# The second score matmul on 128 rows, with projections two pairs of heads ahead

## The reference

```
mod = (silu(c) @ wmod)                          # six vectors per batch
h = layernorm(x) * (1 + ca) + sa
q, k, v = h @ qkv_w.T                           # 16 heads of 64
scores = q k^T / 8 + bias[head, q, k]           # T5 buckets of the distance
x = x + ga * (softmax(scores) v) @ o_w.T
h = layernorm(x) * (1 + cb) + sb
x = x + gb * (routed experts(h) + shared expert(h))   # 160 experts, top 8 by sigmoid
```

## Time and profile before

| | |
|---|---|
| runs (median, range) | 1110.45 us (1110.03 to 1115.24) |
| profiled execution, first to last instruction | 1108.8 us |
| busy: PE, PEld, DVE, ACT | 1067.8, 695.6, 774.9, 729.6 us |
| mean granted TensorE clock | 0.981 |
| attention | about 26 to 615 us |
| experts | about 653 us to the end |

### The profile page before, as it was taken

How to read it: one execution, slowest core, us unless ns; L and a number is a source line. 1 busy time by engine, 2 the same in 40 slices (tenths; PEclk the granted TensorE clock), 3 DMA queues, 4 the chain that set the end, 5 groups by cost and what they waited for, 6 DMA issues and landing times.

```text
span 1108.8 us, 16554 instructions
## 1 busy us (share of the span) xinstructions
PE 1067.8 (96%) x4720; PEld 695.6 (63%) x4720; DVE 774.9 (70%) x1356; ACT 729.6 (66%) x1216; POOL 0.2 (0%) x4
## 2 busy tenths in 40 slices
PE   5999999999999999999999779999999999999998
PEld 2555555555555555555555347788888888888886
DVE  5655555655555555555554558899999999999997
ACT  3566666566665666666665456777777778777775
POOL 0000000000000000000000000000000000000000
PEclk8699999999999999999999899999999999999999
DMA  7651323132231313231321039999999999999993
GB/s 220 193 148 39 77 59 75 44 71 58 75 76 38 76 38 76 57 76 39 76 56 41 1 108 218 218 220 218 218 220 219 218 217 221 218 218 218 221 218 85
DMA packets 60856, 143.63 MB, mean 130 GB/s; under 512 B 8224, under 2 KB 34144, under 8 KB 50704
## 3 DMA queue, kind: packets, MB, share of 16 engines
q1 hardware_dynamic: 60816, 143.18, 57.3%
HBM read 105.60 MB, written 2.42 MB: 97 GB/s over the span
## 4 chain that ended last, share of the span: by engine, by line
PE 92%; DVE 2%; DMA 2%; ACT 1%; issue 1%; SPq 1%; DVEq 0%; ACTq 0%
PE ps L655 37%; PE ps L447 12%; PE ps L462 12%; PE ps L432 10%; PE ps L430 6%; PE ps L403 5%; PE ps L483 3%; PE ps L414 2%; DMA strips<-in_L_ffn_w_down 1%; PE ps L475 1%; SPq L333 1%; DMA comb_rows<-strips 1%; PE ps L573 0%; PE ps L575 0%; PE ps L388 0%
## 5 line engine op out<-in xcount | busy, mean ns | idle before, releaser
L1011 DVE CUSTOM_DVE_ANT_0 s_sb<-ps,strips 128x512 f32<-128x512 f32 x256 | 177.0, 691 | 160.7 <-PE ps L432 152.9
L741 ACT ACTIVATE prob<-s_sb,nmax 128x512 f32<-128x512 f32 x256 | 185.2, 723 | 133.8 <-DVE nmax L1011 133.8
L655 PE MATMUL ps<-hT,wT 128*128 128x512 f32 x960 | 244.1, 390 | 0.3 <-DVE wT L1178 0.3
L1197 DVE TENSOR_TENSOR PT<-v_sb,strips 128x1024 f32<-128x1024 f32 x160 | 195.9, 1224 | 43.6 <-ACT v_sb L881 30.2
L655 PE MATMUL ps<-stack,wT 128*128 128x512 f32 x640 | 198.3, 392 | 9.9 <-DVE wT L1184 9.9
L655 PEld LDWEIGHTS ps<-hT,wT 128*128 128x128 f32 x960 | 180.5, 188 | 39.1 <-ACT strips L856 1.1
L881 ACT ACTIVATE v_sb<-ps 128x1024 f32<-128x1024 f32 x160 | 164.4, 1027 | 48.8 <-PE ps L655 48.3
L1184 DVE TENSOR_TENSOR wT<-PT,stack 128x1024 fp32r<-128x1024 f32 x160 | 195.0, 1219 | 0.0
L873 ACT CAST stack<-PT 128x1024 fp32r<-128x1024 f32 x160 | 166.6, 1041 | 9.1 <-DVE PT L1197 9.1
L447 PEld LDWEIGHTS ps<-ident,prob 128*128 128x128 f32 x1024 | 112.7, 141 | 87.3 <-issue 74.6
L447 PE MATMUL ps<-ident,prob 128*128 128x128 f32 x1024 | 165.7, 285 | 1.5 <-ACT PT L229 1.4
(11 more groups left out here) (106 smaller groups left out, 679.5 us busy)
## 6 DMA issues: line engine op xcount, KB each, us to landing
strips<-comb_rows SPq DMA_DIRECT2D x158, 512.0 KB, 13.4
stack<-qk SPq DMA_DIRECT2D x128, 256.0 KB, 3.8
strips<-bias_rows SPq DMA_DIRECT2D x3, 1792.0 KB, 10.4
strips<-in_L_ffn_w_gate SPq DMA_DIRECT2D x80, 64.0 KB, 12.1
strips<-in_L_ffn_w_down SPq DMA_DIRECT2D x80, 64.0 KB, 14.0
strips<-bias_rows SPq DMA_DIRECT2D x2, 896.0 KB, 5.9
PT<-in_L_attn_qkv_w SPq DMA_DIRECT2D x2, 768.0 KB, 6.7
hcur<-hT SPq DMA_DIRECT2D x3, 512.0 KB, 2.9
```

Of the source, the lines that this page charges most:

```text
L655: last = nc.tensor.matmul(ps[:, bank + c, :], weights(a), rows(m, c), start=start and k == 0, stop=stop and k == 2, skip_group_check=True)
L741: nc.scalar.activation(prob[:, u % 4, :], s_sb[:, u % 2, :], ACT.Exp, bias=nmax[:, u % 4:u % 4 + 1], scale=-1.0, accum_out=rsum[:, n % 2, ...
L1011: nc.vector.tensor_tensor_reduce(out=s_sb[:, u % 2, :], in0=ps[:, BANK_S + u % 2, :], in1=backwards, scale=-1.0, scalar=3.0e38, op0=ALU.ad ...
L1197: nc.vector.tensor_tensor(weighted[:, k % 4, :], silu[:, k % 2, :], cb[:, r, half * HALF:(half + 1) * HALF], ALU.mult).then_inc(s_mul, 1)
```

## The change

- `qkL` is one buffer of one pair (it was two); a new tile `k_low` holds, for each head of an even pair, the low part of the keys on both halves of the partitions; for odd pairs the same is kept in `hT[:, 0]`, which attention does not read after the start (batch 0's input is in `hcur`).
- `stack_pair` issues four more transfers, of 128 KB each, from `qkL` to both halves of that tile: eight for each pair, on the same semaphore.
- The second score matmul (L432) has the first one's 128-row weights from `stack` and `kLow` on 128 rows as its moving operand, so it adds low by low too.
- `project_qk` runs two pairs ahead: pair n makes pair n + 2, after the transposes of unit 6; `qk_high` goes between exponentials 8 and 9, `qk_low` behind copy 7. `project_v` and `copy_v` take the place where the projection and its high copy were. Before pair 0, pair 1 is projected as well. `qk_low` no longer waits for scores of the pair before. The next batch's `hcur` is loaded one pair earlier.

```diff
-    PAIR_STACKED = 4 * 16
+    PAIR_STACKED = 8 * 16
...
-        qk = sb("qk", [P, 6, S], F32R)
-        qkL = qk[:, 0:4, :].rearrange("p (a n) s -> p a n s", a=2)
-        qkH = qk[:, 4:6, :]
+        qk = sb("qk", [P, 4, S], F32R)
+        qkL = qk[:, 0:2, :]
+        qkH = qk[:, 2:4, :]
         stack = sb("stack", [P, 2, 2, 2, S], F32R)
+        k_low = sb("k_low", [P, 2, S], F32R)
+        kLow = (k_low[:, :, :], hT[:, 0, :, :])
...
                 for head, own, other in halves:
                     sp.dma_start(stack[other, par, head, :, :].bitcast(F32),
-                                 qk[own, 2 * par:6:5 - 2 * par, :].bitcast(F32)).then_inc(s_stack[par], 16)
+                                 qk[own, 0:4:3, :].bitcast(F32)).then_inc(s_stack[par], 16)
+                    sp.dma_start(kLow[par][own, head, :].bitcast(F32),
+                                 qkL[own, 1, :].bitcast(F32)).then_inc(s_stack[par], 16)
+                    sp.dma_start(kLow[par][other, head, :].bitcast(F32),
+                                 qkL[own, 1, :].bitcast(F32)).then_inc(s_stack[par], 16)
...
             load_strips(4)
+            stack_pair(0, 3)
...
                 for n in range(2, HPAIRS + 2):
-                    if n == HPAIRS - 1:
+                    if n == HPAIRS - 2:
...
-                    stack_pair(b, n + 1)
+                    stack_pair(b, n + 2)
...
# PE
-                own = slice(head * HD, (head + 1) * HD)
...
-                nc.tensor.matmul(ps[:, BANK_S + g % 2, :], stack[own, par, head, 0, qt * P:(qt + 1) * P],
-                                 qkL[own, par, 1, :], start=False, stop=True).then_inc(s_s, 1)
+                nc.tensor.matmul(ps[:, BANK_S + g % 2, :], stack[:, par, head, 0, qt * P:(qt + 1) * P],
+                                 kLow[par][:, head, :], start=False, stop=True).then_inc(s_s, 1)
...
                 if n >= 1:
                     attend(b, n - 1, 0, final)
-                if not (final and n == HPAIRS - 1):
-                    project_qk(b, n + 1)
+                if n % 2 == 0:
+                    project_v(b, n)
                 transpose_probs(b, n, 1, final)
...
                 transpose_probs(b, n, 4, final)
-                if n % 2 == 0:
-                    project_v(b, n)
                 ahead(7)
...
                 transpose_probs(b, n, 6, final)
+                if not (final and n >= HPAIRS - 2):
+                    project_qk(b, n + 2)
                 if n == HPAIRS + 1:
                     transpose_y(b)
                 ahead(9)
...
             scores(0, 0, 1)
+            project_qk(0, 1)
             pair(0, 0)
...
# ACT
                 copy_probs(b, n, 0)
-                if not (final and n == HPAIRS - 1):
-                    qk_high(b, n + 1)
+                if n % 2 == 0:
+                    copy_v(b, n)
                 copy_probs(b, n, 2)
...
                 copy_probs(b, n, 4)
-                if n % 2 == 0:
-                    copy_v(b, n)
                 ahead(7)
...
                 ahead(8)
+                if not (final and n >= HPAIRS - 2):
+                    qk_high(b, n + 2)
                 ahead(9)
...
# DVE
                 dve.wait_ge(s_qkh, b * HPAIRS + (n + 1))
-                if n >= 2:
-                    dve.wait_ge(s_s, b * G + UNITS * (n - 1))
-                nc.vector.tensor_tensor(qkL[:, n % 2, :, :], ps[:, BANK_PROJ:BANK_PROJ + 2, :],
+                nc.vector.tensor_tensor(qkL[:, :, :], ps[:, BANK_PROJ:BANK_PROJ + 2, :],
...
                 ahead(4)
-                if not (final and n == HPAIRS - 1):
-                    qk_low(b, n + 1)
...
                 copy_probs(b, n, 7)
+                if not (final and n >= HPAIRS - 2):
+                    qk_low(b, n + 2)
                 ahead(10)
```

More of the change, by code:

```diff
@@ L318, in _ @@
                             "p o l s -> p (o l) s").bitcast(F32)).then_inc(ld["hcur"], 16)
-                    stack_pair(b, n + 1)
-            for n in range(2, HPAIRS - 1):
-                stack_pair(B - 1, n + 1)
+                    stack_pair(b, n + 2)
+            for n in range(2, HPAIRS - 2):
+                stack_pair(B - 1, n + 2)
             def load_weights(i, r):
@@ L809, in _ @@
             exponential(0, 0, 1)
+            qk_high(0, 1)
             pair(0, 0)
@@ L1108, in _ @@
             add_bias(0, 0, 2)
+            qk_low(0, 1)
             pair(0, 0)
```

## The result

The changed kernel takes 1053.93 us (median), the one before 1111.24 beside it: a ratio of 0.947 (0.945 to 0.950), 57 us faster. The forecast was 1045, in a range of 1031 to 1069. The profiled execution spans 1052.2 us, 56.6 less than before's 1108.8, against 65 forecast. Lines moved: L438 and L440 are the two score matmuls, L412 is `project_qk`, L423 `project_v`, L455 the transposes, L470 `attend`, L483 `spread_sums`, L491 `project_out`, L1019 the bias, L750 the exponential, L233 the copies, L1004 `qk_low`.

What follows compares the result with a forecast made beforehand. Attention was taken as bound by PE, busy 498.5 of 500 us. Saving 80 less 12 (new wait), 2 (start) and 1 (last pair) gives 65; 1108.8 - 65 + 1.65 was told as 1045 us, range 1031 to 1069.

Steps and rivals of the forecast that it cites:

- Price of the switch, 2.5 us a pair: PE, score matmuls and transposes: one 128-row form saves 2.5 us of 17.2 per pair, 80 us over 32 pairs.
- The drain: PE at L430 to L432: changing tiling mode drains TensorE, so 0.09 goes; without a drain the sum is 40 us smaller.
- The new wait, 0.83: PE, odd pairs: transposes of unit 2 wait 0.83 us for ACT's copy 0; 14 times, 12 us.
- The copies in time: Eight transfers per pair land by 10.4 us, unit 8 of the next pair needs them at 13.2: 2.8 to spare.
- Rival E: Copies land late, unit 8 waits on `s_stack`, the kernel gets slower: 1120 us; chance 0.04.
- Start: First unit at 28.9 us, some 2.4 later; unit 8 of pair 1 at 62 against 65.41; pairs 0 and 1 give 3.
- Pair 2: Pair 2, after the start: forecast to give 2.5 us like other pairs, its copies queued behind two sets of strips.
- in even pairs L414 is put exactly there and hides it: Step of the walk: in even pairs L414, 1.51 us, stands before the transposes and hides the wait for copy 0.
- Rival A: No new wait in odd pairs, the PE saving comes whole: 1033 us; chance 0.15.
- B: Rival: copy 3 or exponentials hold later transposes too, or L430 keeps its 0.09; 15 to 25 us less, 1065; chance 0.24.
- D: Rival: gaps belong to L432's operands, not its rows; PE's 17.2 us per pair stay, 1112 us; chance 0.04.
- C: Rival: L432's weight load cannot run beside L430, so 0.11 stays 256 times, 28 us less, 1073; chance 0.03.

Runs made afterwards that it cites:

- e3: The changed kernel with ACT's copy 0 moved ahead of the exponential of unit 3; 1036.92 us, ratio 0.935 to the kernel before.
- e1: The changed kernel with its second score matmul back on the head's own 64 rows, copies and order kept; 1111.8 us, ratio 1.003 to the kernel before.
- e8: The changed kernel with copy 0 first, strips loaded later, and PE's unit 5 scores moved ahead of the second attend; 1024.02 us, ratio 0.922.
- e4: The changed kernel with DVE's `qk_low` moved one place, behind the bias of unit 10; 1051.43 us, ratio 0.947 to the kernel before.
- e2: The changed kernel with projections and `hcur` loads back at the old places, one pair ahead; 1097.06 us, ratio 0.990 to the kernel before.

## Why the prediction was right

- *Price of the switch, 2.5 us a pair.* Right. Measured 2.4: even pairs 18.60 to 16.19, odd pairs 17.18 to 14.85 once their wait is out (e3). L438 takes 0.31 to 0.32 after transposes (0.31 forecast), L440 0.23. The bound on the L430 term (0.09 might stay) fell. e1 shows the cause: taking the rows back takes all of it back.
- *The drain.* The Trainium skill's rule ("TensorEngine Tiling (Array Packing)", section Tiling Modes: a change of mode drains TensorE) agrees with these runs, in which the 0.09 goes with the change of form; that it is a drain, the rows cannot show. A change in columns costs as well: e8 has one group of 64 columns fewer between full ones, and 0.35 us less a pair.
- *The new wait, 0.83.* Right in place and cause, 0.71 in size (e3, e4); 14 of them 10 us instead of 12.
- *The copies in time.* Right: from 100 to 550 us no wait of PE is ended by a DMA. With the margin taken away (e2) unit 8 waits 0.5 to 2.5 us for them. Rival E was close, though. In the changed kernel the last of a pair's copies is issued at 123.83 us, its unit starts at 129.43, and in e2 PE went on 3.4 to 3.7 us after the start of that issue: some 2 us to spare, where 2.8 were forecast.
- *Start.* The first unit came 3.1 us later (2.4 forecast), unit 8 of pair 1 at 63.16 (62). That the lead at pair 2 (2.3 us) came near the 3 forecast is in part luck: the 65.41 from which it is counted has in it the 10 us at a clock of 0.50.
- *Pair 2.* Missed, 2.7 us. I had counted the late landing at 62 but not what followed it. Some 1.6 us are the stretch of lower clock (63.16 to 67.94 is 4.78 us, the same in e3 3.20), which no walk of the orders can give; 1.1 are a wait for copy 0, which even pairs were said not to have, behind the eight small operations of `sign_gates` on DVE:

```profile
74.92 0.66 PE L455 MATMUL ps<-ident,prob 128*128 128x128 f32 x4 [0.98 <-ACT PT L233]
```

- *Behind the turns.* Missed, 3.5 us. The step that failed is "in even pairs L414 is put exactly there and hides it". It does, unless DVE is later still: there the update of x and the statistics stand in its row, and 1.5 us of issue follow at two of the three turns. The kernel before shows such an idle time at its turn, and I read only pairs inside a batch. Its DVE, in order of time:

```profile
217.09 0.69 DVE L1011 CUSTOM_DVE_ANT_0 s_sb<-ps,strips 128x512 f32<-128x512 f32 x1 [2.26 <-issue]
```

The forecast's terms add up to 65.4 before rounding, against 56.6. The start gave 2.3 instead of 3 (0.7 less), pair 2 lost 0.2 instead of giving 2.5 (2.7 less), the pairs behind the turns gave 4.0 instead of 7.5 (3.5 less), the other 25 pairs 2.0 less, and the last pair 1.7 instead of 1.5. In the 25, two errors partly cancel: the switch is worth 2.3 and not 2.5 in the 14 odd pairs (2.5 us), and their wait is shorter (1.7 us back).

The forecast's own sign of being wrong, periods above 16.5 us, did show, in pair 2 (18.97) and behind the turns (18.86, 18.83 and 17.39), and there even pairs have the wait as well; in the rest the periods are those forecast. Rival A (no wait) was wrong. B's time was off by 11 us and the forecast's by 9, so the time alone would not part them; the rows do, since copy 3 and the exponentials before T5 and T6 were in time and L438 lost its 0.09. D is refuted by 0.23 and by e1, C by 0.23. C's rule, from the Trainium skill's "TensorE: Matmul & The Clock Gate", section "The mechanism", that loads overlap matmuls in flight only with another row group, does not hold for L440: its load (191 ns) goes to the same 128 rows as L438's matmul and costs nothing. The same section excepts loads into a background weight buffer, which would allow it; no run here shows where the load goes.

## What to carry to other kernels

Where PE is full, look at starts and not at durations. In this kernel each change between full matmuls and those on part of the rows or columns costs about 0.1 us on leaving a form and 0.1 on entering the next, and a narrow group between full ones makes two such changes: 0.35 to 0.4 us. So it can pay to multiply twice the rows, or to put narrow matmuls side by side. A faster engine uses up the slack of everything that feeds it (here the copies' landing and the place of one copy on ACT), so walk one period of each engine's order with the new durations, and then the pairs that differ: the first ones, and the one behind each turn of a loop. The cheapest gain after the change was one line on another engine.

## What the hardware showed that I had not expected

- The gap of 1.5 us on "issue" on DVE at a loop's turn, and that the same code in a line runs 0.06 to 0.12 us slower in every pair of 15.6 to 16.2 us. In the kernel before, whose pairs are longer, the last batch is written out too and takes the same 17.2 and 18.6 us as the loop.
- A wait of PE of about 2 us is sometimes followed by some 3 us at the lower clock, and mostly not: it was behind 2.24 us in the changed kernel (0.56) and behind 3 of 15 such waits in e2, and it was not behind 2.85 us in e3 or 2.14 us in e4. One trace of each kernel does not say whether a gain at such a place is the edit's or the clock's.
